# A recurrent block and six windowed attention layers on one core: the output projection, layer norm and feed forward moved two steps later in the turn

## The reference, cut to what matters

```python
q, k, v = split(x @ Wqkv)                       # 16 heads of 64
q = rotary(l2norm(q) * qs); k = rotary(l2norm(k) * ksc)
p = softmax(q k^T * 8, in windows of 32)        # own and previous window
x = x + (p @ v) @ Wo
y = shift_tokens(x)                             # half of the channels come from the token before
xn = (y - mean(y)) / sqrt(var(y) + 1e-5) * g + b
a, gate = split(xn @ W1 + b1)                   # 341 columns each
x = x + (a * gelu(gate)) @ W2 + b2
```

## Time and profile before

| | |
|---|---|
| median of three runs | 3610.63 us |
| the profiled execution | 3610.49 us |
| its span, first to last instruction | 3608.7 us |
| mean granted TensorE clock | 0.996 of full speed |
| busy: PE, DVE, ACT, POOL | 91%, 84%, 83%, 80% |
| state space block, before the first turn | about the first 330 us |
| DMA, mean over the span | 110 GB/s |

### The profile page before, as it was taken

The page is one execution under the profiler, slowest core; times in us unless marked ns, Lnnn a source line. Parts: engine busy times, 40 slices in busy tenths (PEclk is TensorE's granted clock), DMA queues, the critical chain, the costliest instruction groups (busy, mean ns, idle before and its releaser), DMA issues.

```text
span 3608.7 us, 92500 instructions
## 1 busy us (share of the span) xinstructions
PE 3292.0 (91%) x29710; PEld 2114.4 (59%) x29710; DVE 3038.7 (84%) x10488; ACT 3011.2 (83%) x8812; POOL 2879.2 (80%) x2383
## 2 busy tenths in 40 slices
PE   7887899999999999999999999999999999999998
PEld 3444566656666556666656666656666666666665
DVE  7997888888888888888888888888888888888886
ACT  6554888888888888888888888888888888888887
POOL 6787887887887887887888887888887887887883
PEclk9999999999999999999999999999999999999999
DMA  5443323333323333322333322333322333332322
GB/s 167 136 133 123 110 101 103 105 115 105 115 102 103 104 113 104 115 101 102 107 114 106 116 102 100 108 116 103 116 103 98 108 115 105 115 104 98 107 101 92
DMA packets 261726, 396.22 MB, mean 110 GB/s; under 512 B 45566, under 2 KB 86588, under 8 KB 261244
## 3 DMA queue, kind: packets, MB, share of 16 engines
q1 hardware_dynamic: 261244, 390.30, 32.2%
HBM read 157.91 MB, written 6.03 MB: 45 GB/s over the span
## 4 chain that ended last, share of the span: by engine, by line
PE 47%; ACT 30%; DVE 13%; issue 7%; POOL 2%; DMA 0%; DVEq 0%; ACTq 0%; SPq 0%; POOLq 0%
ACT pr L1182 13%; PE bank L884 9%; PE bank L873 7%; PE bank L844 5%; PE bank L360 4%; PE bank L362 4%; PE bank L912 4%; PE bank L361 4%; ACT sq L1170 4%; DVE ab L1608 3%; DVE wide L1500 3%; PE bank L854 3%; PE bank L829 2%; DVE sm L1656 2%; PE bank L855 2%
## 5 line engine op out<-in xcount | busy, mean ns | idle before, releaser
L1182 ACT ACTIVATE pr<-sm,nb,rq 128x128 f32<-128x128 f32 (+1 forms) x3072 | 1518.3, 501 | 159.2 <-DVE nb L1667 158.3
L1343 POOL TENSOR_TENSOR pr<-pr,rden 128x640 f32<-128x640 f32 x768 | 964.9, 1256 | 492.5 <-DVE rden L1633 488.5
L1357 POOL TENSOR_TENSOR rot<-ab,swp 128x512 f32<-128x512 f32 x760 | 977.2, 1286 | 78.9 <-DMA swp<-ab 78.2
L1608 DVE TENSOR_TENSOR ab<-bank,ltab 128x1024 f32<-128x1024 f32 x760 | 925.4, 1218 | 92.1 <-PE bank L362 83.4
L1656 DVE CUSTOM_DVE_ANT_0 sm<-bank,mask 128x128 f32<-128x128 f32 (+1 forms) x3072 | 766.0, 302 | 119.4 <-ACT pr L1182 113.3
L1182 ACT ACTIVATION_READ_ACCUMULATOR pr<-sm,nb,rq 128x1 f32 x3072 | 597.3, 194 | 0.0
L1170 ACT ACTIVATE sq<-bank 128x512 f32<-128x512 f32 x768 | 453.9, 591 | 101.2 <-DVE ab L1608 95.0
L1643 DVE COPY pt<-bank 128x512 f32<-128x512 f32 x768 | 529.5, 689 | 9.9 <-PE bank L855 2.8
L854 PE MATMUL bank<-ident,pr 128*128 128x128 f32 x1536 | 397.9, 286 | 142.7 <-DVE pt L1643 142.5
L1363 POOL TENSOR_TENSOR rot<-rot,rkb 128x512 f32<-128x512 f32 x384 | 493.2, 1290 | 21.4 <-DMA rkb<-k_scratch 21.0
L873 PE MATMUL bank<-pt,vtok 128*64 128x160 f32 (+1 forms) x6144 | 461.1, 292 | 52.2 <-ACT vtok L1196 52.2
(11 more groups left out here) (213 smaller groups left out, 5700.4 us busy)
## 6 DMA issues: line engine op xcount, KB each, us to landing
swp<-ab SPq DMA_DIRECT2D x1520, 128.0 KB, 2.1
rkb<-k_scratch SPq DMA_DIRECT2D x768, 128.0 KB, 2.9
rot<-c_scratch SPq DMA_DIRECT2D x64, 256.0 KB, 3.3
sq<-c_scratch SPq DMA_DIRECT2D x64, 256.0 KB, 3.2
xs<-xT SPq DMA_DIRECT2D x95, 128.0 KB, 2.3
xs<-xT SPq DMA_DIRECT2D x95, 127.5 KB, 2.4
raw<-Wqkv SPq DMA_DIRECT2D x48, 128.0 KB, 2.6
wo<-Wo SPq DMA_DIRECT2D x6, 512.0 KB, 4.5
```

What stands on the lines that cost most here:

```text
L1182: ins = act.activation(pr[:, s % 4, i, t, 0:P + WINDOW * t], sm[:, s % 2, i, cs], ACT.Exp, bias=nb[:, s, t, i:i + 1], scale=head_scale(rq, ...
L1343: ins = pool.tensor_tensor(pr[:, e % 4, :, :, :], pr[:, e % 4, :, :, :], rden[:, e, :, :].rearrange("p t i -> p i t").unsqueeze(3) .to_bro ...
L1357: pool.tensor_tensor(rot[:, PAIRS * (j % 2) + j // 2, :], ab_of(j, 0, lead), swp_of(j, lead), ALU.add).then_inc(qk_rot, 1)
L1608: dve.tensor_tensor(ab_both(j, lead).rearrange("p i (b t) -> p i b t", b=GB), seqs(qk_bank(j, lead)[:, :]).unsqueeze(1).to_broadcast(shape ...
```

## The change

The output projection, the layer norm, and the feed forward's gelu, gates and down projection stand two steps later (the gelu two, the gates and the down projection two or three). The parts `a` of the up projection leave steps 14 and 15 for steps 0, 1 and 2 of the turn after. Banks are dealt anew: blocks 0 to 5, 7, 9 and 11 to 15 use bank 5, the others bank 6. The last two sums of squares stand in step 1 of the turn after, and the ring of squares has nine places. Layer norm's product with the reciprocal deviation and the gain is one operation of DVE that reads the centred x from its bank, so ACT makes no Copy; the bias is added by ACT in the rounding (L1270) and again by DVE in `low`. POOL makes none of them. Layer norm's Ln and Exp stand on their own in step 10, after the square of that step.

```diff
-NSQ = 8
+NSQ = 9
-BANK_STEPS = [[('prev2', 'dn', 0, 4), ('next', 'qk', 0, 5)], [('next', 'qk', 1, 5)], [('prev', 'wo', 0, 6), ('next', 'qk', 2, 5)],
- [('next', 'qk', 3, 5)], [('cur', 'rqT', 1, 4), ('next', 'qk', 4, 7)], [('next', 'qk', 5, 5)],
- [('next', 'sum', 0, 7), ('next', 'qk', 6, 4)], [('next', 'qk', 7, 5)],
- [('next', 'qk', 8, 4), ('prev', 'cen', 0, 6), ('prev', 'var', 0, 6)], [('next', 'qk', 9, 5)],
- [('next', 'qk', 10, 4)], [('next', 'rqT', 0, 6), ('next', 'qk', 11, 5)],
- [('prev', 'g', 0, 4), ('next', 'qk', 12, 5)], [('prev', 'g', 1, 6), ('next', 'qk', 13, 5)],
- [('prev', 'g', 2, 7), ('next', 'qk', 14, 5), ('prev', 'a', 0, 6), ('next', 'sum', 1, 7), ('prev', 'a', 1, 4)],
- [('prev', 'a', 2, 6), ('next', 'qk', 15, 5)]]
+BANK_STEPS = [[('next', 'qk', 0, 5), ('prev2', 'a', 0, 4)], [('next', 'qk', 1, 5), ('prev2', 'a', 1, 6), ('cur', 'sum', 1, 7)],
+ [('next', 'qk', 2, 5), ('prev2', 'a', 2, 4)], [('prev2', 'dn', 0, 6), ('next', 'qk', 3, 5)],
+ [('prev', 'wo', 0, 4), ('cur', 'rqT', 1, 7), ('next', 'qk', 4, 5)], [('next', 'qk', 5, 5)],
+ [('next', 'sum', 0, 7), ('next', 'qk', 6, 6)], [('next', 'qk', 7, 5)], [('next', 'qk', 8, 6)], [('next', 'qk', 9, 5)],
+ [('prev', 'cen', 0, 4), ('next', 'qk', 10, 6), ('prev', 'var', 0, 7)], [('next', 'qk', 11, 5)],
+ [('next', 'rqT', 0, 6), ('next', 'qk', 12, 5)], [('next', 'qk', 13, 5)],
+ [('prev', 'g', 0, 4), ('next', 'qk', 14, 5)], [('prev', 'g', 1, 6), ('next', 'qk', 15, 5), ('prev', 'g', 2, 7)]]
-AT = {'wo': 2, 'shift': 5, 'residual': 6, 'centred': 7, 'ln_k': 8, 'norm': 10, 'high': 10, 'low': 11, 'gelu': 13,
- 'gated': (15, 15, 16), 'down': (16, 17, 19), 'residual2': 19, 'scale_q': (11, 4), ...
+AT = {'wo': 4, 'shift': 7, 'residual': 8, 'centred': 9, 'ln_k': 8, 'ln_n': 10, 'norm': 11, 'high': 12, 'low': 13, 'gelu': 15,
+ 'gated': (17, 18, 18), 'down': (19, 20, 21), 'residual2': 21, 'scale_q': (13, 5), ...
-QUAD_STEPS = {8: ('next', 1), 0: ('cur', 3)}
+QUAD_STEPS = {8: ('next', 1), 1: ('cur', 3)}
 SPREAD_STEPS = {0: ('cur', 3), ...
- 4: ('cur', 5)}
+ 5: ('cur', 5)}
 SCALE_STEPS = {13: [('cur', 7)],
+ 0: [('cur', 1)],
  1: [('cur', 2)],
+ 4: [('cur', 3)],
+ 5: [('cur', 4)],
  7: [('cur', 5)],
  9: [('cur', 6)],
- 14: [('next', 0), ('next', 1)],
- 2: [('cur', 3)],
- 5: [('cur', 4)]}
+ 14: [('next', 0)]}
...
 @ ScalarE, def square
-                    if j % 4 == 0 and (cur is not None or j >= 8):
+                    if j % 4 == 1 and (cur is not None or j >= 9):
 @ ScalarE, the loop over s
-                        act.activation(xn, use_bank("cen", 0)[:, :], ACT.Copy).then_inc(f_xc, 1)
-                        norms(0, nxt, prev)
+                        norms(0, nxt, None)
+                    if s == AT["ln_n"] and prev is not None and kind != "drain":
+                        norms(0, None, prev)
                     if s == AT["high"] and prev is not None and kind != "drain":
-                        act.activation(xn_h[:, :], xn, ACT.Copy).then_inc(f_hi, 1)
+                        act.activation(xn_h[:, :], xn, ACT.Identity, bias=lv[:, V_B:V_B + 1]).then_inc(f_hi, 1)
 @ GpSimd
-                def normed(q):
-                    pool.tensor_tensor(xn, xn, xv, ALU.mult).then_inc(f_xn, 1)
-                    pool.tensor_scalar(xn, xn, lv[:, V_G:V_G + 1], lv[:, V_B:V_B + 1], ALU.mult, ALU.add)
-                def low(q):
-                    pool.tensor_tensor(xn_l[:, :], xn, xn_h[:, :].bitcast(F32), ALU.subtract).then_inc(f_split, 1)
 @ VectorE
+                def normed(q):
+                    dve.wait_ge(f_cen, n1 + (q + 1))
+                    dve.wait_ge(f_rstd, n1 + (q + 1))
+                    dve.scalar_tensor_tensor(xn, use_bank("cen", 0)[:, :], lv[:, V_G:V_G + 1], xv, ALU.mult, ALU.mult).then_inc(f_gb, 1)
+                def low(q):
+                    dve.wait_ge(f_hi, n1 + (q + 1))
+                    dve.scalar_tensor_tensor(xn_l[:, :], xn, lv[:, V_B:V_B + 1], xn_h[:, :].bitcast(F32),
+                                             ALU.add, ALU.subtract).then_inc(f_split, 1)
 @ VectorE, the loop over s, behind gated and ahead of clamp and the maxima
+                    if s == AT["norm"] and prev is not None and kind != "drain":
+                        normed(prev)
+                    if s == AT["low"] and prev is not None and kind != "drain":
+                        low(prev)
```

More of the change, by code:

```diff
@@ L77 @@
 NWO = 4
-BACK = {"load": 10, "silu": {1: (0, 4), 3: (4, 7)}, "mul": 4, "halves": 3, "before": 2, "between": 4, "add": (8, 10, 11), "store": 12}
+BACK = {"load": 10, "silu": {1: (0, 4), 5: (4, 7)}, "mul": 6, "halves": 3, "before": 2, "between": 4, "add": (8, 10, 11), "store": 12}
 BACK_BANKS = (0, 1, 2, 3, 5)
[L80 to L84, removed]
- 'ln_k': 8,
[L86 to L92, removed]
+LAST_BANKS = {"cen": (7, 4), "var": (6, 7), "dn": (6, 7), "out": (2, 3)}
@@ L93 @@
+AT = {'wo': 4,
+ 'shift': 7,
+ 'residual': 8,
+ 'centred': 9,
+ 'ln_k': 8,
+ 'ln_n': 10,
+ 'norm': 11,
+ 'high': 12,
+ 'low': 13,
+ 'gelu': 15,
+ 'gated': (17, 18, 18),
+ 'down': (19, 20, 21),
+ 'residual2': 21,
  'clamp': (9, 2),
- 'scale_q': (11, 4),
+ 'scale_q': (13, 5),
  'k_out': (9, 2),
@@ L268, in build @@
         xs_in, xs2_in, cen_halves = sem("xs_in"), sem("xs2_in"), sem("cen_halves")
[L269 to L270 removed]
+        f_cen, f_xc, f_sq, f_var, f_ln, f_rstd, f_gb, f_hi, f_split = (
+            sem(f"f_{n}") for n in ("cen", "xc", "sq", "var", "ln", "rstd", "gb", "hi", "split"))
         f_g, f_gelu, f_a, f_h, f_dn, f_add = (sem(f"f_{n}") for n in ("g", "gelu", "a", "h", "dn", "add"))
@@ L829, in square_sums @@
                         mm = pe.matmul(bank[7][32 * t:32 * t + 32, :], headsum[:, k % 2, :],
-                                       sq[:, (4 * k + t) % NSQ, :], start=(k % 2 == 0), stop=(k % 2 == 1),
+                                       sq[:, (n16 - CREDIT + 16 * q + 4 * k + t) % NSQ, :], start=(k % 2 == 0), stop=(k % 2 == 1),
                                        skip_group_check=True)
@@ L1167, in square @@
                     act.wait_ge(qk_mul, n16 + (16 * q + j + 1))
-                    if j % 4 == 0 and (cur is not None or j >= 8):
+                    if j % 4 == 1 and (cur is not None or j >= 9):
                         act.wait_ge(sq_part, n4 + (4 * q + j // 4 - 1))
-                    act.activation(sq[:, j % NSQ, :], qk_bank(j, first)[:, :], ACT.Square).then_inc(qk_sq, 1)
+                    act.activation(sq[:, (n16 - CREDIT + 16 * q + j) % NSQ, :], qk_bank(j, first)[:, :], ACT.Square).then_inc(qk_sq, 1)
                 def probabilities(s):
@@ L1224, in gelu @@
                     act.preload_act_table_set("silu_and_others" if kind == "drain" else "natural_log_exp_and_others")
-                if kind == "T2":
-                    act.wait_ge(f_a, n3 - 3)
-                    split_high(nl, 6)
                 if prev is None and cur is not None:
@@ L1248, in turn @@
                         norms(1, cur, None)
-                    if kind == "T2" and s == 1:
+                    if kind == "T2" and s == 3:
+                        act.wait_ge(f_a, n3 - 3)
+                        split_high(nl, 6)
+                    if kind == "T2" and s == 4:
                         split_high(nl, 7)
@@ L1265, in turn @@
                         split_high_x(par)
-                    if s == AT["ln_k"] and (nxt is not None or prev is not None) and kind != "drain":
-                        norms(0, nxt, prev)
+                    if s == AT["ln_k"] and nxt is not None and kind != "drain":
+                        norms(0, nxt, None)
+                    if s == AT["ln_n"] and prev is not None and kind != "drain":
+                        norms(0, None, prev)
                     if s == AT["high"] and prev is not None and kind != "drain":
                         act.wait_ge(f_gb, n1 + (prev + 1))
-                        act.activation(xn_h[:, :], xn, ACT.Copy).then_inc(f_hi, 1)
+                        act.activation(xn_h[:, :], xn, ACT.Identity, bias=lv[:, V_B:V_B + 1]).then_inc(f_hi, 1)
                     if kind == "drain" and s in BACK["silu"]:
@@ L1400, in turn @@
                         split_low(nl, SPLIT_AT[kind][s - 1])
-                    if kind == "T2" and s in (1, 2):
-                        split_low(nl, 5 + s)
+                    if kind == "T2" and s in (4, 5):
+                        split_low(nl, 2 + s)
                     for role, p in SCALE_STEPS.get(s, ()):
@@ L1407, in turn @@
                         split_low_x(par)
-                    if prev is not None and kind != "drain":
-                        if s == AT["norm"]:
-                            normed(prev)
-                        if s == AT["low"]:
-                            low(prev)
             pool.wait_ge(lv_ok, 1)
```

19 lines of the change are left out of this document (5 added, 14 removed).

## The result

The changed kernel takes 4271.86 us (median of four, 4268.56 to 4275.94), beside 3610.39 us for the kernel before: 1.183 times as long, 95% interval 1.181 to 1.185, or +661 us. The forecast was 4010 us and its range ended at 4080 us. Direction and main cause hold; the size does not.

The account below looks back on a forecast made before the run. A turn was taken as PE's steps plus ACT and DVE's steps plus the gelu step; 7.5 + 1.0 + 5.9 + 8.0 + 23.4 + 3.0 + 27.3 = 76.1 us, +8.7 us over some 46 turns: 4010 us, range 3740 to 4080 us.

Parts of the forecast that it names:

- The tie of the engines: Most q and k blocks share bank 5, so PE projects a block only after ACT has squared the one before.
- The rivals without this stall: No gate stall, 3813 us (chance 0.17); two steps exchanged alone, 3700 us (0.08); PE fills gaps, 3587 us (0.07).
- The signs named: Turn 75 to 77 us; third gate idle near 180 us; PE waiting before block 3; `normed` waiting; ACT idle.
- t(0) to P(1): From the end of ACT's square 0 to the end of PE's projection of block 1: 1.0 us per turn.
- P(1) to P(2): From the end of PE's projection of block 1 to that of block 2: 5.9 us of PE work.
- P(3) to P(8): From the end of PE's projection of block 3 to that of block 8: 23.4 us of PE work.
- the chain from P(2) to square 2: From PE's end of block 2 through gate, maxima, bias, exponentials and norm operations to ACT's square's end: 7.0 us.
- The gate term: Third gate waits for its `a` in step 2: blocks 2 to 3 take 8.0 us, +4.3 us per turn.
- t(8) to t(15): From the end of ACT's square 8 to that of square 15: 27.3 us per turn.
- The stretch of ACT and DVE: Steps 9 to 15, where ACT and DVE rule and PE waits: 27.3 us per turn after the change.
- The relief of POOL: POOL loses three layer norm operations; costed at nothing because nobody waits long for POOL.
- The lock at full price: Rival: DVE and POOL's shared port lock adds another 1.3 us on `low`, giving 4070 us; chance 0.08.

## Why the prediction was right, and where it was wrong

**The tie of the engines, and the gate.** Right. `a` 2 in the step of its own gate makes DVE, ACT and PE wait in turn; taking the gate one step later removes it (-267 us), and planting it in the kernel before brings it there (+150 us). The rivals without this stall (3813, 3700 and 3587 us) fall. The signs named were seen: 242.7 us at the third gate (180 named), `normed` waiting 94.4 / 47 = 2.0 us for Exp (1 to 2 named), ACT idle 4.18 us ahead of the exponentials of step 2. One sign was not: PE's long wait is not ahead of block 3 but two entries earlier, ahead of the transposes, for DVE's copy, which stands behind the same gate; what is left ahead of block 3 is 0.44 us.

**The terms at the whole clock.** t(0) to P(1) 1.0, P(1) to P(2) 5.8 and P(3) to P(8) 23.6 us, for 1.0, 5.9 and 23.4 predicted (the parts of the last one, as the prediction lists them, add up to 23.8, so it holds a slip of 0.4 us, about 18 us in all); the chain from P(2) to square 2 took 7.28 us for 7.0. The gate term, 8.0, is 8.3 at the whole clock.

**The step that failed: the sum, 76.1 us per turn, where 82.1 were measured.** Two of its terms were mis-sized.

*A PE pause was costed at its own length alone*, and the lower clock behind it at nothing. The stretches of before show a clock of 1.00 throughout, and the sum took that for granted through a change that opens pauses of 1.5 to 3.4 us in PE's work. By the table the slower matmuls on the path cost 0.5 (t(0) to P(1)), 0.8 (P(1) to P(2)), 0.6 (P(2) to P(3), by the run with PE filled), 0.9 (P(3) to P(8)) and 0.6 us (t(8) to t(15)): 3.4 us per turn, some 156 us. Filling one of the pauses gave back 43 us; the 156 are an estimate from turns with and without, and no run took all of it away. The 0.6 us of t(8) to t(15) are the least certain: a turn that stalls longer there may be the one whose clock falls, and with the lower level nearly gone from that stretch (the run with extra work in steps 12 to 14) it was no shorter.

*The stretch of ACT and DVE, 27.3 us, is 29.8 at the whole clock.* The medians of its steps 9 to 15 are 5.2, 3.4, 5.0, 3.8, 4.8, 4.3 and 3.0 us, for 4.9, 3.5, 4.8, 3.5, 4.1, 3.5 and 2.95. The largest misses are steps 13 and 14. Step 13 has `low`, which took 1.24 us and not 0.65 + 0.2. The prediction had kept another 1.3 us for it in the range, and about 0.4 of that came. Step 14 was priced by ACT, 3.5 us; in the timeline above it is DVE that has no gap from one pair of products to the next, 1523.40 to 1527.73, 4.33 us: the products, eight maxima, two biases (one held, 0.67 us) and the copy. Less the hold, 3.8 us is what a full even step costs DVE, and ACT's price was the wrong one of two. That exchanging 14 and 15 into this stretch was dear was seen; how dear was not.

Together: 3.4 for the clock, 2.5 for this stretch, 0.3 for the gate and small terms of both signs make the 6.0 us that were missing, 276 us over 46 turns; 262 us lie between forecast and result.

**What I cost at nothing.** The relief of POOL was put at nothing, and that was wrong in the order of before: the biases of step 12 are held 0.5 us less per turn, and the step is shorter by about as much. Together with the Copy's 0.5 us it stayed hidden behind the late sum; with the sum early enough both showed, 0.7 us per turn. In the changed kernel no run separates it. The lock at full price as a rival, 4070 us, had its mechanism in the trace and, on `low`, a third of its size; the bias held in step 14 is the same mechanism, 0.5 us there, where no term had it.

**The range.** It ended where its dearest known term ended. All its cases priced a stall as idle time, so none could reach 4272 us.

## What to carry to other kernels

Before an operation is moved in a hand-written turn, list for every in-order queue what stands behind each new wait, and put a consumer a step behind its producer: one due time too early was worth 267 us here. Where PE rules at full clock, ask of every new pause also what the matmuls after it will cost at the lower level, and add that to the sum. Price a step by each engine that could set it and take the largest; an operation that is removed may have been the cover of a wait, so look at what comes next before calling it a gain.
